# A four-phase graph kernel on one core: the 125-node chunk moved to second place, x asked for at once, the fourth phase's own term taken from DRAM

## What is computed

```python
h = jnp.maximum(_layernorm(x, axis=-1), 0.0)
x = x + _L0_gnn_ref(h, src, dst, ...)
h = jnp.maximum(_layernorm(x, axis=-1), 0.0)
x = x + _L1_gnn_ref(h, edge_index, ...)

# L0: twice, with a relu between and log_softmax behind
agg = jax.ops.segment_sum(h[edge_src], edge_dst, num_segments=n) * inv_deg
y = jnp.concatenate([h, agg], axis=1) @ W + b
# L1: two convolutions with relu, then two dense layers
h = relu(mean @ W_l.T + b_l + h @ W_r.T)
h = relu(h @ W_lin1.T + b_lin1)
h = h @ W_lin2.T + b_lin2
```

## Time and profile before

| | |
|---|---|
| runs | 600.82 us, median of 3 (600.31 to 601.1) |
| profiled execution | 599.37 us, its span 597.6 us |
| TensorE matmul busy | 554.2 us (93% of the span) |
| VectorE, ScalarE, GpSimd busy | 218.6, 215.9, 24.0 us |
| share of the chain of waits | TensorE 86%, VectorE 5%, ScalarE 3%, DMA 2% |

### The profile page before, as it was taken

The page is one execution under the profiler, slowest core; times in us unless marked ns, Lnnn a source line. Parts: engine busy times, 40 slices in busy tenths (PEclk is TensorE's granted clock), DMA queues, the critical chain, the costliest instruction groups (busy, mean ns, idle before and its releaser), DMA issues.

```text
span 597.6 us, 9565 instructions
## 1 busy us (share of the span) xinstructions
PE 554.2 (93%) x3131; PEld 294.3 (49%) x3131; DVE 218.6 (37%) x489; ACT 215.9 (36%) x391; POOL 24.0 (4%) x34
## 2 busy tenths in 40 slices
PE   1457999999999999999999999999999999999996
PEld 0244655555554654445455555544544445454454
DVE  6888968577774227667311111100100001010000
ACT  1588857577674204454432212101101110111021
POOL 4320000000000000101100000000000000000000
PEclk9999999999999999999999999999999999999999
DMA  3700103010010133332110000200110202010011
GB/s 94 190 2 1 37 1 114 2 35 17 17 34 18 23 90 97 94 103 54 40 29 18 17 17 5 93 21 0 21 32 1 50 0 51 0 38 13 6 33 28
DMA packets 27421, 22.99 MB, mean 38 GB/s; under 512 B 4143, under 2 KB 26928, under 8 KB 27264
## 3 DMA queue, kind: packets, MB, share of 16 engines
q1 hardware_dynamic: 25670, 21.45, 13.5%
q10 hardware_dynamic: 1561, 0.84, 0.5%
q0 software_dynamic: 160, 0.33, 0.3%
HBM read 16.42 MB, written 6.19 MB: 38 GB/s over the span
## 4 chain that ended last, share of the span: by engine, by line
PE 86%; DVE 5%; ACT 3%; DMA 2%; issue 2%; POOL 1%; ACTq 0%; DVEq 0%; SPq 0%; POOLq 0%
PE ps L1011 53%; PE ps L1028 23%; PE ps L965 5%; PE ps L1021 2%; DVE hs_b L473 1%; DMA adj<-key_d,adj 1%; ACT hs_b L774 1%; PE ps L1245 1%; ACT adj L1481 1%; DMA invc<-inv_d 1%; POOL adj L1357 1%; PE ps L1217 1%; POOL adj L1364 1%; DVE adj L1408 1%; PE ps L1291 1%
## 5 line engine op out<-in xcount | busy, mean ns | idle before, releaser
L1011 PE MATMUL ps<-adj,hs_b 125*128 (+2 forms) x1050 | 205.7, 351 | 0.0
L1011 PE MATMUL ps<-adj,hs_a 125*128 (+2 forms) x700 | 158.6, 353 | 0.0
L1011 PEld LDWEIGHTS ps<-adj,hs_b 125*128 125x128 f16 x1050 | 95.9, 97 | 105.4 <-issue 9.9
L473 DVE TENSOR_TENSOR hs_b<-iota,hs_b 128x1024 f16<-128x1024 f16 x150 | 95.9, 686 | 29.6 <-PE ps L965 28.0
L965 PE MATMUL ps<-hs_b 128*128 128x125 f16 x625 | 69.4, 235 | 21.4 <-DVE hs_b L473 13.4
L813 ACT ACTIVATE adj<-ps 125x500 f32 (+2 forms) x150 | 80.2, 543 | 23.6 <-PE ps L965 17.3
L965 PEld LDWEIGHTS ps<-hs_b 128*128 128x128 f16 x625 | 46.7, 104 | 67.2 <-DVE hs_b L473 34.7
L1011 PEld LDWEIGHTS ps<-adj,hs_a 125*128 125x128 f16 x700 | 58.6, 98 | 38.8 <-issue 5.4
L763 DVE TENSOR_TENSOR hs_a<-ps,hs_a 125x512 f32<-125x512 f32 (+1 forms) x7 | 4.4, 634 | 170.3 <-PE ps L1291 170.3
L1028 PE MATMUL ps<-aggT,wts 128*128 128x500 f32 (+1 forms) x112 | 44.6, 540 | 0.4 <-ACT aggT L924 0.4
L1028 PE MATMUL ps<-aggT,hs_a 128*128 128x500 f32 (+1 forms) x84 | 35.1, 540 | 0.5 <-ACT aggT L952 0.5
(11 more groups left out here) (152 smaller groups left out, 358.8 us busy)
## 6 DMA issues: line engine op xcount, KB each, us to landing
invc<-inv_d SPq DMA_DIRECT2D x24, 250.0 KB, 3.3
self_d<-hs_b SPq DMA_DIRECT2D x6, 250.0 KB, 2.0
hs_b<-self_d SPq DMA_DIRECT2D x6, 250.0 KB, 3.5
hs_b<-in_x_dram SPq DMA_DIRECT2D x6, 250.0 KB
x_d<-hs_b SPq DMA_DIRECT2D x6, 250.0 KB
hs_a<-x_d SPq DMA_DIRECT2D x6, 250.0 KB
out_dram<-hs_a SPq DMA_DIRECT2D x6, 250.0 KB
wt_d<-adj SPq DMA_DIRECT2D x1, 1152.0 KB, 4.2
```

What stands on the lines that cost most here:

```text
L473: last = nc.vector.tensor_tensor(onehots[slot], iota2.unsqueeze(1).to_broadcast(shape), keys[:, ds(g * 4, 4), :].unsqueeze(2).to_broadcast ...
L1011: last = nc.tensor.matmul(acc[:, 0:n], hs[:, ds(s * (2 * w) + part * w + h * 128, 128)], adj[0:P, ds(c * (S * C) + s * n, n)], start=(isin ...
```

## The change

- Prologue: all of x is asked for on ScalarE's queue at once. `norm` stops at tile 16 in the prologue; tiles 17 to 24 and `weights_act` are done in `first1`.
- Counting: chunk 6's 25 windows are grouped in fours, as six groups of four and one of one (GR = 7). Its groups follow chunk 0's.
- First phase: the order is 0, 6, 1, 2, 3, 4, 5. `first1` aggregates chunk 0 and counts chunk 6; the step of chunk 6 counts chunk 1, and so on; the step of chunk 5 counts nothing. `place(c)` gives a chunk's turn, `first_group(c)` its first group's number. Chunk 5's dense work lies in the first step of the second phase, which takes source tile 24 in 17th place.
- Third phase: SP writes `actT` to DRAM (`h3_d`) for each chunk; ScalarE waits for that before it writes `actT` again.
- Fourth phase: `own4` and its two copies go; `h3T` is loaded from `h3_d` (`load_h3`). `lin2` makes nodes the rows at once, as eight matmuls of 128 columns, so that `turn4` and ScalarE's copy of its input go; the bias is added by VectorE to x1. A chunk's first half waits for the eviction of bank 0, its second half for that of bank 1.

```diff
+GR = 7
 ...
+            if slow or (isinstance(c, int) and c == 0):
+                return c
+            if isinstance(c, int) and c == NFULL:
+                return 1
+            return c + 1
+        def first_group(c):
+            if isinstance(c, int) and c in (0, NFULL):
+                return S if c else 0
+            return c * S + GR
...
# prologue, SP and ScalarE
-            sp.wait_ge(sem("gathered0"), 16)
-            for a, b in WHOLE16:
-                sp.dma_start(tiles(xs0[a:b, XA * D:S * D], D), x[XA * P:N, :]...)
+            for t0, t1, name in ((0, XA, "x_in_a"), (XA, S, "x_in_b")):
+                for a, b in WHOLE16:
+                    act.dma_start(tiles(xs0[a:b, t0 * D:t1 * D], D), x[t0 * P:t1 * P, :]...)
...
# first phase, VectorE
             def first1():
-                build_a(1, True)
-                lows(2)
-                build_b(1, True)
-                belows()
-                build_c(1, True, 0, 1)
-                lows(3)
-                build_c(1, True, 1, 3)
-                lows(4)
-                degrees_of_windows()
-                build_c(1, True, 3, 7)
+                build_rest(0, 2)
+                belows()
+                lows(2)
+                build_rest(2, 5)
+                lows(3)
+                degrees_of_windows()
+                build_rest(5, GR)
+                lows(4)
...
# first phase, TensorE
                 for i in range(S):
-                    count(S + i, i, True, S + i - 1)
+                    if i < GR:
+                        count(S + i, i, S + i - 1, n_w=GW if i < GR - 1 else 1)
...
-                    if i == 8:
+                    if i == 4:
                         window_sums(pe)
...
-                step1(1, True, True, second=True)
-                with pe.Fori(2, NFULL - 1) as c:
-                    step1(c, True, True)
-                step1(NFULL - 1, True, False)
-                step1(NFULL, False, None)
+                step1(NFULL, False, 1, 0, True, second=True)
+                step1(1, True, 2, NFULL, False)
+                step1(2, True, 3, 1, True)
+                with pe.Fori(3, NFULL - 1) as c:
+                    step1(c, True, c + 1, c - 1, True)
+                step1(NFULL - 1, True, None, NFULL - 2, True)
...
# third phase, SP
+                sp.wait_ge(sem("p3_relu"), 2 * c + 2)
+                sp.dma_start(h3_d[:, :, ds(c * C, n)], actT...).then_inc(sem("p3_h3_out"), 16)
...
# fourth phase, TensorE
-                        if at == 0 and ph > 2 and not done:
-                            wait_past(pe, f"p{ph}_agg_out", len(aggs) * c)
+                        if at % S == 0 and ph > 2 and at >= done:
+                            wait_past(pe, f"p{ph}_agg_out", len(aggs) * (c - 1) + at // S + 1)
...
             def lin2(c, full):
-                dense(2, n, [(bv[:, k, :], aggT[:, k * C:k * C + n]) for k in range(2)])
-            def turn4(c, full):
+                for t in range(n // P):
+                    for k in range(2):
+                        last = nc.tensor.matmul(bank(2, 4 * D, P)[:, t * D:(t + 1) * D],
+                                                aggT[:, k * C + t * P:k * C + (t + 1) * P],
+                                                bv[:, k, :], start=(k == 0), stop=(k == 1))
-                   [(0, own4, 1), (10, hidden4, 1), (20, lin1, 1), (30, lin2, 1), (40, turn4, 1)],
+                   [(10, hidden4, 1), (20, lin1, 1), (30, lin2, 1)],
```

More of the change, by code:

```diff
@@ L465, in pe_slow, with group @@
             return last
-        def group(g, slot, full, wait):
+        def group(g, slot, quad_of, wait):
             wait_past(nc.vector, "counted", wait)
-            if full:
+            if quad_of is not None:
                 shape = [128, 4, 128, 2]
                 last = nc.vector.tensor_tensor(onehots[slot], iota2.unsqueeze(1).to_broadcast(shape),
-                                               keys[:, ds(g * 4, 4), :].unsqueeze(2).to_broadcast(shape), ALU.is_equal)
+                                               keys[:, ds(quad_of * 4, 4), :].unsqueeze(2).to_broadcast(shape), ALU.is_equal)
             else:
@@ L872, in first1, with step1, counted @@
-            def first1():
-                build(1, True, 0, 8)
+            def step1(nxt, prev, prev_full, before, before_full=True):
+                def counted(a, b):
+                    if nxt is not None:
+                        build(nxt, True, a, b)
+                h0_turned(prev, prev_full)
+                if before is not None:
+                    high(before, before_full)
+                counted(0, CUT1)
+                if before is None:
+                    turned_out(act, 1, 3)
+                relu(prev, prev_full)
+                counted(CUT1, CUT2)
+                z_out(prev, prev_full)
+                if before is None:
+                    counted(CUT2, 16)
+                    turned_out(act, 2, 3)
+                    counted(16, S - 1)
+                else:
+                    counted(CUT2, S - 1)
@@ new lines, in rest_group @@
+            def rest_group(i):
+                nd = C // S if i < GR - 1 else WD
+                act.wait_ge(sem("counted"), S + i + 1)
+                nc.scalar.activation(columns(NFULL, False, i * (C // S), nd),
+                                     bank(i % 2, nd * S, P).rearrange("p (d t) -> p t d", t=S), ACT.Copy).then_inc(
+                    sem("evicted"), 1)
+            def first1():
+                rest_group(0)
+                rest_group(1)
+                norm(act, 17, 20)
+                rest_group(2)
+                rest_group(3)
+                norm(act, 20, 25)
+                rest_group(4)
+                rest_group(5)
+                rest_group(6)
@@ L885, in act_layers @@
+                for k in (1, 2):
+                    turned_out(act, k, 3)
                 chunks(act, whole)
@@ L963, in count @@
             slot = (i - 1) % 3 if i else SLOT0
-            for w in range(GW if c_full else 1):
-                last = nc.tensor.matmul(bank(i % 2 if b is None else b)[:, w * WD * S:(w + 1) * WD * S], onehots[slot][:, w // 2, :, w % 2],
+            for w in range(n_w):
+                last = nc.tensor.matmul(bank(i % 2 if b is None else b)[:, w * WD * S:(w + 1) * WD * S],
+                                        onehots[slot][:, w // 2, :, w % 2],
                                         onehots[slot][:, 2 + w // 2, 0:WD * S, w % 2], start=True, stop=True)
@@ L1180, in step0 @@
                     ahead = 0
+                    late = (17, 21) if order else ((NFULL - 1) * (C // P), S - 1)
                     for at in range(len(aggs) * S):
@@ L1190, in step0 @@
                                 pe.wait_ge(sem(f"p{ph - 1}_low"), source[1 + k])
-                        tile(0, True, at)
+                        tile(0, True, at, order and order[at])
                 def step(c, full):
@@ L1256, in pe_layers @@
             h3T = wts[:, 0:2 * C]
-            def own4(c, full):
-                wait_past(pe, "p4_lin2T", c)
-                own(hbz, H, 0, 2, c, full).then_inc(sem("p4_own"), 1)
-                wait_past(pe, "p4_sum", c)
-                own(hbz, H, 1, 3, c, full).then_inc(sem("p4_own"), 1)
             def hidden4(c, full):
@@ L1297, in pe_layers @@
             if not slow:
-                for part in (own4, hidden4, lin1, lin2, turn4):
+                for part in (hidden4, lin1, lin2):
                     part(NFULL, False)
```

285 lines of the change are left out of this document (150 added, 135 removed).

## The result

The change takes **596.52 us** (median of 5 runs, 595.52 to 598.03); the kernel before, measured with it, 600.31 (599.13 to 601.10). The ratio is 0.9937, with a 95% interval from 0.9916 to 0.9959. It is faster, by 3.8 us where I had forecast 10.8, and lies just above my range. The profiled execution took 595.76, of which 593.9 are its span (before: 599.37 and 597.6), so the two traces differ by 3.7.

A forecast was written before the change was run, and what follows sets the result against it. TensorE, busy 93% of the span, was taken to bound the four phases, and waits over DMA, VectorE and ScalarE the prologue. Terms -7.2 + 3.9 + 0.9 - 8.4 = -10.8 took 600.82 to 590.0 us; range 585.0 to 596.5.

The forecast's parts named there:

- I charge it nothing: Prologue: the 0.2 MB key write, now meeting x, costs nothing; served behind all of x, the sum is 1.5 us smaller.
- That wait goes. It would then be free at 21.9: Prologue: VectorE's 2.51 us wait for the keys, until 24.40, disappears; no more than 2.5 us can come from here.
- the held keys: Prologue rival: x and the key write share the engines, first gathers wait; prologue gains only 3.5, total 593.7; chance 0.14.
- first1: First phase, chunk 0 aggregated while chunk 6 is counted: 15.8 us, to 59.7, with the moved norm tiles hidden.
- The step of chunk 6, 24.3: First phase: VectorE is the limit against TensorE's 18.3 us of work; the step takes 24.3 us, to 84.0.
- it can run only three groups ahead, so it waits about 4 us: Chunk 6 step: VectorE, limited to three groups ahead, waits about 4 us while TensorE is in its two dense parts.
- the falling clock: Chunk 6 step rival: TensorE's clock falls, dense runs and next first tiles partly at half speed; +3, 593.0; chance 0.20.
- The chunk 1 step: First phase, with chunk 6's small dense work: 18.4 us plus the 1.1 an ordinary step loses, to 103.5.
- the rest to the second phase: From the end of chunks 0, 6, 1 to the second phase's `turn2` of chunk 0: -6.8 us.
- Third phase 0: Third phase: SP's store of the 0.5 MB relu, awaited by ScalarE a whole step later, costs nothing.
- Fourth phase -8.4: Fourth phase: 7.9 us saved without `own4` and `turn4`, 0.6 lost in `lin2`, 1.1 gained at the end.
- its rival: Fourth phase: `lin2` runs at the speed of its weight loads, +7.5 us, total 597.4; chance 0.06.

The follow-up runs named there:

- e4: The change with the second part of x asked for on SP's queue right behind the key write, not on ScalarE's: 596.05 us, ratio 0.9927.
- e7: The change with the second part of x back on SyncE's queue behind the first gather of keys: 597.50 us, ratio 0.9958.
- e5: The change with TensorE's bounds taken at tile 20 of chunk 0's aggregation and VectorE's scale worked out before chunk 0's sums are scaled: 591.89 us.
- e1: The kernel before with only the change's third- and fourth-phase edits: 591.09 us, ratio 0.9838.
- e10: e5 with thirteen of chunk 1's groups counted from tile 12 of chunk 0 on, `hidden1` moved behind tile 12: 589.73 us, ratio 0.9827.
- e15: e14 with the second part of x on SyncE's queue behind the key write, as in e4: 588.95 us, ratio 0.9813.
- e13: e10 with the bounds at tile 14 and VectorE's arithmetic on them behind comparison 6 of chunk 1, not 12: 590.11 us, ratio 0.9844.
- e14: e13 with five small extra matmuls in each gap behind counts at the prologue's end and in `first1`: 590.86 us, ratio 0.9841.
- e16: The change with the same small extra matmuls as e14 and nothing else: 596.96 us, ratio 0.9951.

## Why the prediction missed

The direction was right, four of five stage sums were right to 2.8 us or better, and one was wrong by 6.3.

- **"I charge it nothing"** is the first step that failed. The key write, issued behind x's start, made the first gather 3.06 us late (e4 and e7 undo exactly that). I had the last gather landing near 19; its data were used at 22.00. The gathers that wait for the write started at 14.12, later than even my bound of 12.5 for its landing; the DMA engines' share had fallen to 0.42 from 11 us on. The Trainium skill ("DMA: Bandwidth & Descriptors", queues, rings and completion order) has engines take turns packet by packet, from which I had made an estimate of 1 us; the delay of 3.06 us doesn't agree with that estimate. The page counts packets and I had counted bytes, so the case speaks against my estimate and not for sure against the rule.
- **"That wait goes. It would then be free at 21.9"**: VectorE's second split came at 24.94. Everything behind it was right: I had 22.0 us from there to the first count (21.9 to 43.9), three profiles show 21.8. So the miss of 2.8 in the prologue is that one time, and the held keys are 1.8 of it: in e4, with the keys in time, the split still comes at 23.17, because TensorE's four counts and VectorE's own work stand ahead of it. And -4.4 needed no early x at all: e7 has it without. It is ScalarE's shed work.
- **`first1`**: 16.9 us for 15.8. The detour over the window sums was right: TensorE waits 1.68 behind them. Of the extra 1.1, 0.54 is a wait for an eviction that queues behind the moved norm tiles, which I had called hidden.
- **The step of chunk 6, 24.3** measured 30.1, the largest term of the miss. What failed is the clause "it can run only three groups ahead, so it waits about 4 us". VectorE's work was priced well: my terms make 19.8 without the wait, and it was busy 20.15 us in the step. But it stood idle for 10.0 us and not for 4: 6.2 of them, in two waits, behind the two dense parts alone, and the rest mostly around the bounds. I had paired its waits with the dense parts at full clock, and overlooked that the 2.3 us of bounds stand *in front of* comparisons, at the one place where TensorE has no stock of them. That is 1.8 us; the falling clock came with it, a rival priced at +3 and measured at 2.9 in the first dense part. The rest, about one microsecond, is not traced to one cause; ScalarE's evictions, which my sum has nowhere, end half of TensorE's waits. That e5 takes 24.3 as well is luck: it has the 2.3 us of bounds outside the step (VectorE is busy 16.3 us and idle 8.0). My terms as written make 23.8, too, and not 24.3.
- **The chunk 1 step** 18.8 for 19.5, **the rest to the second phase** -7.5 for -6.8: right. TensorE's wait there grew from 0.26 to 1.08, as forecast.
- **Third phase 0**: right, 0.0. The 500 KB stores land in 3.1 us and cost nothing that the stage's time shows.
- **Fourth phase -8.4** measured -9.6, and -9.5 alone in e1. `lin2` took 1.75 where I had 1.78, so its rival is dead. A step fell from 34.34 to 32.94 us, 1.4, where I had 1.2; six steps make the difference.

So two rivals came true together, held keys and falling clock, each in the place I gave. The clock's price was near (2.9 in the dense part for 3). The held keys' price was not: I had 3.7 us for them, and e4, which frees them, brings the first count 1.8 us forward and the whole by 0.5, which is no more than the noise. That I had forecast the pair at 596.6, against 596.52, is therefore luck: the chunks 0, 6 and 1 were 6.3 us off and the prologue 2.8, and the fourth phase and the stretch before it gave 1.9 more than forecast. The weights were too low as well: 0.14 and 0.20 for things for which a row spoke, and nothing for the two together.

## What to carry to other kernels

When an edit reorders stages so that a lean one stands where a full one stood, write down who fills its buffers and what else that engine has to do in it: here 2.3 us of small arithmetic on VectorE cost TensorE 1.8 us of waiting and then 2.9 us more for a dense part at half clock, and moving it gave back 4.6. Count every engine of the round, the one that empties the banks too. Before asking for a large transfer earlier, look what small write on another queue is on the critical path then. And run a change's independent parts alone: here one part was worth 9.5 us and the rest cost 5.4.

## What the runs showed of the hardware

- A 0.2 MB write on one queue, issued while 1.6 MB ran on another at 207 to 241 GB/s, delayed what waited for it by 3.06 us. In eleven other kernels with the same order of transfers the delay was 2.2 (e10) to 3.8 us (e5). With the second 1.0 MB of them behind the write on its own queue (e4, e15), it was delayed by nothing.
- In the change the granted clock fell to 0.50 behind a stretch of short groups of matmuls with a wait of 1.81 us in it (TensorE busy 1.24 us of 66 to 68, 0.55 of 68 to 70), and a dense part then took 6.30 us for 3.35. In e13 TensorE waited 1.55 us between long groups (busy 1.42 of 62 to 64, 2.00 of 66 to 68), and the clock stayed at 1.00. With five matmuls of 128 columns in each gap of the prologue's end and of `first1` it stayed at 1.00 there (e14, e16). The Trainium skill ("TensorE: Matmul & The Clock Gate", the second HAM failure mode) says that frequent short idles between groups of matmuls make the clock swing; the change's trace agrees.
- The first tiles behind the prologue took 0.83 instead of 0.42 us in the kernel before while the granted clock read 1.00; in the change the same tiles took as long and the clock read 0.50; in e14, with TensorE kept busy, they took 0.42. The row of the clock doesn't show all of it, and why it read full before stays open.
- Runs of one kernel spread by up to 4.7 us, and with the mean clock (e13: 588.61 at 0.996, 593.29 at 0.987), while the kernel before, whose mean clock reads 0.997 or more, spreads by 2.5 at most in one session.
